# Gate and up products in two passes over x1, and the first normalisation's statistics one slot later: one post-norm layer on one core

## The chip, the cores and the metric

The kernel runs on one core of a Trainium2 chip. TensorE, VectorE (DVE in the rows), ScalarE (ACT), GpSimd (POOL) and SyncE (SP) each work through a queue of their own in order, and meet at semaphores. The metric is the device time of one execution in microseconds. The time before is the median of three runs.

## The reference, cut to what matters

For each of 16 sequences of 256 rows by 256 columns, all in fp32:

```python
qkv = x @ Wqkv + bqkv                      # 16 query heads, 4 key/value heads of 16
prob = softmax(q k^T / 16)
x1 = layernorm(x + (prob v) @ Wout + bout)
gate, up = split(x1 @ ternary(w_gate_up).T)      # 1024 columns each
h = silu(gate) * up
y = rms_norm(h) @ ternary(w_proj).T
out = layernorm(x1 + y)
```

The ternary weights are made in the kernel at its start. Products that need fp32 accuracy are made from two fast ones: an operand is split into a rounded high part and the rest, its low part.

## The kernel before

The work is a pipeline of slots. One sequence takes eight slots of issue, and 172 slots in all are run; sequence b passes through stage `OFFSET` in slot 8b + OFFSET. Slots 0 to 63 and 128 to the end are written out, those between are a hardware loop whose body is 16 slots. A slot is the same list of "if this stage is due" blocks on every engine, so the order of the blocks in an engine's `slot` function is the order of its queue. What is called slot residue r below is the slot whose number is r modulo 8.

Every slot, if its stage is running, does one eighth of the attention of a sequence (two score products for the row maxima, the scores again for the exponential, every second slot the product with v) and one eighth of the feed-forward of an earlier sequence:

- TensorE, `gate_up` (line 507): eight matmuls 128x128 by 128x256 into one PSUM bank `ffn_ps`, gate in one half and up in the other. It waits for `x1T_lo` (the low part of x1 transposed) and for `h_done` of the slot before, since `ffn_ps` is single.
- ScalarE: tanh of the gate half, and behind it in its queue the exponential, then `h_hi` of the slot before.
- DVE: row maximum 0, then `gated` and `h_f` (lines 817 and 824), then row maximum 1.
- GpSimd (line 924 on), first in the slot: `h_lo` and, behind it, the running sum `sq_sum` of the slot before. Then, if due, `LN2_APPLY` (the final output `y_out` of the sequence two before, two instructions), then `RSTD1`, then others.

The first normalisation is made once in eight slots. In residue 3 (offset 27) TensorE makes the output projection; DVE at the end of that slot adds the residual (`r1`, line 890), takes `bn_stats` twice and `bn_aggr` twice; GpSimd, at the end of its slot, makes `rstd1` in two small instructions (lines 944 and 922). In residue 4 (offset 28) DVE, behind row maximum 1, applies it (`LN1_APPLY`, line 881, two instructions that make `x1`). In residue 5 TensorE transposes x1 (line 613; its PSUM bank is the one of that slot's row maximum 0) between the product with v and `down`; ScalarE makes `x1T_hi`. In residue 6 DVE makes `x1T_lo` (line 765) behind `h_f`. In residue 7 the first `gate_up` of the sequence uses both. `LN2_APPLY` has offset 44, so it falls in residue 4 too.

The GpSimd queue around it:

```python
if st := n.once(LN2_APPLY):          # 44
    wait(pool, rstd2_done, st.count(1, 1))
    ...                              # two tensor_scalar of 128x256
if st := n.once(RSTD1):              # 27
    wait(pool, var1_done, st.count(TT, TT))
    pool.tensor_tensor(ve1[:], mv1[:, :, 1], ln_eps[:], ALU.add)
    wait(pool, ve1_done, st.count(1, 1))
    rsqrt(rstd1[:], ve1[:], rstd1_done)
```

Of the kernel before, what the change touches and what calls it, by code (L numbers as in the profile page):

```python
# [24 lines left out]
P = 128  # L25
# [3 lines left out]
F = 4 * D  # L29
TT = S // P  # L30
DT = D // P
# [43 lines left out]
PV_DIVIDE = (22, 24)  # L75
ATT_HIGH = 26
O_ADD = 27
RSTD1 = 27
X1_HIGH = 29
X1_LOW = 30  # L80
GATE0 = 31
# [85 lines left out]
def wait(eng, sem, value):  # L167

    if isinstance(value, int):
        if value > 0:  # L170
            eng.wait_ge(sem, value)
    else:
        eng.wait_ge(sem, value)
# [26 lines left out]
def postln_layer(nc, x, Wqkv, bqkv, Wout, bout, w_gate_up, w_proj, out):  # L200
    ctx = ExitStack()
    with ctx:
        def sb(name, shape, dt=F32):
            return ctx.enter_context(nc.sbuf_tensor(name, shape, dt))
# [4 lines left out]
        def sem(name):  # L209
            return ctx.enter_context(nc.semaphore(name))  # L210
# [14 lines left out]
        wguT = sb("wguT", [P, DT, 2 * F], F32R)  # L225
# [37 lines left out]
        r1 = sb("r1", [P, TT, D])  # L263
        st1 = sb("st1", [P, TT, 6])
        mv1 = sb("mv1", [P, TT, 2])
# [3 lines left out]
        x1T = [sb(f"x1T_{n}", [P, 2, DT, S], F32R) for n in ("hi", "lo")]  # L269
# [23 lines left out]
        def short(n, name):  # L293
# [30 lines left out]
        r1_done, bn1_done, var1_done, ve1_done, rstd1_done, x1_done = (  # L324
            sem("r1_done"), sem("bn1_done"), sem("var1_done"), sem("ve1_done"), sem("rstd1_done"), sem("x1_done"))
        x1_turned, x1T_hi, x1T_lo = sem("x1_turned"), sem("x1T_hi"), sem("x1T_lo")
# [6 lines left out]
        waited, sp_waited, pool_waited = sem("waited"), sem("sp_waited"), sem("pool_waited")  # L333
# [16 lines left out]
        def alternate(n, st):  # L350

            return n.it is None and n.t >= TWO_BANKS and st.s % 2 == 1

        def gate_up_bank(n, st, half):
            return exp_ps[:, half, 0:S] if alternate(n, st) else ffn_ps[:, half, :]
# [86 lines left out]
        def _(pe):  # L442
            def products(dst, lhs, rhs, start=True, stop=True):

                pairs = list(zip(lhs, rhs))
                for i, (a, b) in enumerate(pairs):
                    last = pe.matmul(dst, a, b, start=start and i == 0, stop=stop and i == len(pairs) - 1)  # L447
                return last
# [56 lines left out]
                last.then_inc(exp_scored, 1)  # L505

            def gate_up(n, st):
                wait(pe, x1T_lo, st.count(1, 1))
                if st.it is None and st.b == 0 and st.s == 0:
                    pe.wait_ge(w_ev, len(pieces))  # L510
                if alternate(n, st) and n.t - SLOTS < TWO_BANKS and st.s == 1:
                    wait(pe, exp_done, SLOTS * B)
                wait(pe, h_done, st.count(8, st.s - 1 if n.it is None and n.t > TWO_BANKS else st.s))
                for half in range(2):
                    c = half * F + st.s * P
                    last = products(gate_up_bank(n, st, half),
                                    [wguT[:, k, c:c + P] for k in range(DT) for _ in range(2)],
                                    [x1T[a][:, st.par, k, :] for k in range(DT) for a in range(2)])
                last.then_inc(ffn_made, 1)

            def down(st):
# [48 lines left out]
            def slot(n):  # L570
                if st := n.chunk(FFN0):
                    gate_up(n, st)
# [187 lines left out]
        def _(dve):  # L760
# [3 lines left out]
            def low(dst, src, hi):  # L764
                return dve.tensor_tensor(dst, src, hi.bitcast(F32), ALU.subtract)  # L765

            def both(n, name):
                return short(n, name)[:].rearrange("p (k t) -> p k t", k=2)
# [42 lines left out]
            def slot(n):  # L811
# [7 lines left out]
                if st := n.chunk(H0):  # L819

                    wait(dve, gated_done, st.count(8, st.s + 1))
                    wait(dve, h_lo, st.count(8, st.s - 1))
                    wait(dve, h_squared, st.count(8, st.s - 1))
                    dve.tensor_tensor(h_f[:, st.s % 2, :], gated[:, st.s % 2, :], gate_up_bank(n, st, 0), ALU.mult  # L824
                                      ).then_inc(h_done, 1)
                if st := n.once(X1_LOW):
                    wait(dve, x1T_hi, st.count(1, 1))
                    low(x1T[1][:, st.par], both(n, "x1"), x1T[0][:, st.par]).then_inc(x1T_lo, 1)
# [41 lines left out]
                if st := n.once(V_COPY):  # L870
# [4 lines left out]
                    for t in range(TT):  # L875
                        last = dve.tensor_copy(v_ones[:, st.par, t, :, 0:HD], v[:, t, 1])
# [10 lines left out]
                if st := n.once(O_ADD):  # L887
                    wait(dve, o_made, st.count(1, 1))
                    wait(dve, bout_added, st.count(1, 1))
                    dve.tensor_tensor(r1[:], both(n, "o"), res[:, st.par], ALU.add).then_inc(r1_done, 1)  # L890
                    wait(dve, r1_done, st.count(1, 1))
                    for t in range(TT):
                        dve.bn_stats(st1[:, t, :], r1[:, t, :]).then_inc(bn1_done, 1)  # L893
                    wait(dve, bn1_done, st.count(TT, TT))
                    dve.sem_inc(waited, 1)
                    for t in range(TT):
                        dve.bn_aggr(mv1[:, t, :], st1[:, t, :]).then_inc(var1_done, 1)
                if st := n.once(K_LOW):
                    wait(dve, k_copied, st.count(1, 1))
                    low(k_p[:, 1, :], kv_f[0:KV, :], k_p[:, 0, :]).then_inc(k_lo, 1)  # L900

            run_slots(dve, slot)


        @block.gpsimd
        def _(pool):
# [17 lines left out]
            def slot(n):  # L924
# [10 lines left out]
                if st := n.once(LN2_APPLY):  # L935
# [3 lines left out]
                    for t in range(TT):  # L939
                        pool.tensor_scalar(y_out[:, st.par, t, :], r2[:, t, :], mv2[:, t, 0:1], rstd2[:, t:t + 1],  # L940
                                          ALU.subtract, ALU.mult).then_inc(y_done, 1)
                if st := n.once(RSTD1):
                    wait(pool, var1_done, st.count(TT, TT))
# [53 lines left out]
```

## Time and profile before

| | |
|---|---|
| median of three runs | 621.06 us (619.04 to 621.45) |
| profiled execution | 616.0 us, of it 614.1 us span |
| mean granted TensorE clock | 0.971 |
| TensorE matmul busy | 554.9 us, 90% of the span |
| TensorE weight load busy | 467.1 us, 76% |
| DVE busy | 442.1 us, 72% |
| ScalarE busy | 369.9 us, 60% |
| GpSimd busy | 327.6 us, 53% |

An engine's busy time is a sum over the whole span. Which wait ends last in which slot has to be read from the timeline. Between sequences the steady part repeats every 32.8 us.

### The profile page before, as it was taken

Reading aid. Unit: us, or ns where it says so; the run is one execution under the profiler, and the core shown is the slowest. Engines: PE = TensorE matmul, PEld = TensorE weight load, DVE = VectorE, ACT = ScalarE, POOL = GpSimd, SP = SyncE. Lnnn points to the kernel's source line nnn. Section 1 sums busy time; section 2 is a strip of 40 time slices with the busy share of each in tenths; the row PEclk is TensorE's granted clock in tenths of the full one; section 3 lists DMA queues with packets and bytes.
Section 4 is the critical chain, followed back from the end, with each engine's and each line's share of the span. In section 5 each row is a group of like instructions: output and inputs, shape, how many; then the busy total and the mean of one; then the engine's idle time right before and its main releaser. Section 6 shows DMA issues by size and latency. Waiting matters only on the chain.

```text
span 614.1 us, 14165 instructions
## 1 busy us (share of the span) xinstructions
PE 554.9 (90%) x4368; PEld 467.1 (76%) x4368; DVE 442.1 (72%) x1034; ACT 369.9 (60%) x738; POOL 327.6 (53%) x436
## 2 busy tenths in 40 slices
PE   5768979999999999999999999999999999999782
PEld 5657768778888887878787888788887877777772
DVE  7885875777777777786777777877777787855751
ACT  4453745576666666757566666666666756566441
POOL 5432331243645555555637473646555555566975
PEclk9687999999999999999999999999999999999996
DMA  6963454454352617062534435342617070101001
GB/s 226 159 139 45 84 83 89 79 97 70 77 107 59 124 45 139 4 148 37 136 47 103 78 77 103 78 104 63 119 44 138 23 141 4 36 2 36 18 1 35
DMA packets 53932, 49.08 MB, mean 80 GB/s; under 512 B 6144, under 2 KB 53888, under 8 KB 53888
## 3 DMA queue, kind: packets, MB, share of 16 engines
q1 hardware_dynamic: 51152, 47.60, 37.8%
q10 hardware_dynamic: 2736, 0.92, 0.7%
q8 instruction: 24, 0.39, 0.3%
q14 instruction: 20, 0.16, 0.1%
HBM read 33.29 MB, written 14.68 MB: 78 GB/s over the span
## 4 chain that ended last, share of the span: by engine, by line
PE 68%; DVE 20%; issue 5%; POOL 3%; ACT 1%; DMA 1%; ACTq 0%; POOLq 0%; DVEq 0%; SPq 0%
PE ffn_ps L447 17%; PE short_ps L447 11%; PE pv_ps L544 10%; PE short_ps L494 8%; PE down_ps L529 7%; PE exp_ps L503 7%; PE short_ps L552 5%; DVE w_hat L809 3%; DVE row_max L776 3%; DVE gated L817 2%; DVE st L893 2%; DVE r L890 2%; DVE x1T_lo L765 2%; DVE h_f L824 1%; DVE w_sum L793 1%
## 5 line engine op out<-in xcount | busy, mean ns | idle before, releaser
L776 DVE TENSOR_REDUCE row_max<-short_ps 128x2 f32<-128x512 f32 x256 | 173.7, 682 | 64.5 <-PE short_ps L494 64.4
L928 POOL TENSOR_TENSOR h_lo<-h_f,h_hi 128x256 fp32r<-128x256 f32 x128 | 94.6, 739 | 191.2 <-ACT h_hi L672 180.9
L690 ACT ACTIVATE probs<-exp_ps 128x1024 f32<-128x1024 f32 x128 | 130.9, 1023 | 37.3 <-PE exp_ps L503 34.0
L447 PE MATMUL ffn_ps<-x1T_hi,wguT 128*128 128x256 f32 x480 | 125.0, 293 | 15.9 <-DVE h_f L824 9.0
L494 PE MATMUL short_ps<-k_st,q_st 65*128 65x256 f32 x512 | 116.5, 309 | 13.0 <-DVE row_max L776 12.7
L447 PE MATMUL ffn_ps<-x1T_lo,wguT 128*128 128x256 f32 x480 | 119.3, 282 | 0.0
L681 ACT ACTIVATE tanh<-ffn_ps 128x256 f32<-128x256 f32 x120 | 45.8, 382 | 118.9 <-PE ffn_ps L447 101.9
L447 PEld LDWEIGHTS ffn_ps<-x1T_hi,wguT 128*128 128x128 f32 x480 | 90.8, 189 | 23.0 <-DVE h_f L824 11.1
L494 PEld LDWEIGHTS short_ps<-k_st,q_st 65*128 65x128 f32 x512 | 82.1, 192 | 23.6 <-DVE row_max L776 11.1
L447 PEld LDWEIGHTS ffn_ps<-x1T_lo,wguT 128*128 128x128 f32 x480 | 91.0, 189 | 0.0
L933 POOL TENSOR_TENSOR sq_sum<-sq_sum,h_sq 128x256 f32<-128x256 f32 x112 | 83.2, 743 | 0.0
L529 PE MATMUL down_ps<-wpT,h_hi 128*128 128x256 f32 x256 | 76.2, 320 | 5.9 <-POOL h_lo L928 5.9
L503 PE MATMUL exp_ps<-q_st,k_st 67*128 67x512 f32 x256 | 81.4, 399 | 0.2
L544 PE MATMUL pv_ps<-probs,v_ones 128*32 128x256 f32 x1024 | 68.5, 385 | 0.0
L529 PE MATMUL down_ps<-wpT,h_lo 128*128 128x256 f32 x256 | 66.8, 283 | 0.0
L529 PEld LDWEIGHTS down_ps<-wpT,h_hi 128*128 128x128 f32 x256 | 48.8, 191 | 19.5 <-issue 11.5
L817 DVE SCALAR_TENSOR_TENSOR gated<-tanh,ffn_ps 128x256 f32<-128x256 f32 x120 | 49.3, 410 | 18.9 <-ACT tanh L681 18.9
L824 DVE TENSOR_TENSOR h_f<-gated,ffn_ps 128x256 f32<-128x256 f32 x120 | 50.5, 421 | 5.4 <-DVE gated L817 1.6
L672 ACT ACTIVATE h_hi<-h_f 128x256 fp32r<-128x256 f32 x128 | 52.3, 409 | 1.2 <-DVE h_f L824 1.2
L529 PEld LDWEIGHTS down_ps<-wpT,h_lo 128*128 128x128 f32 x256 | 49.0, 191 | 0.4
L447 PE MATMUL short_ps<-xT,wqkv 128*128 128x256 f32 x192 | 48.2, 388 | 0.0
L722 ACT ACTIVATE h_sq<-h_f 128x256 f32<-128x256 f32 x112 | 45.7, 408 | 0.0
(98 smaller groups left out, 892.7 us busy)
## 6 DMA issues: line engine op xcount, KB each, us to landing
q_st<-q_dram SPq DMA_DIRECT2D x128, 128.0 KB, 4.1
q_dram<-q_p SPq DMA_DIRECT2D x16, 512.0 KB, 3.0
xn<-in_L_attn_x_dram SPq DMA_DIRECT2D x16, 256.0 KB, 4.5
k_st<-k_dram SPq DMA_DIRECT2D x64, 64.0 KB, 2.6
res<-in_L_attn_x_dram SPq DMA_DIRECT2D x16, 256.0 KB, 3.2
out_dram<-y_out SPq DMA_DIRECT2D x16, 256.0 KB, 2.2
wgu_raw<-in_L_ffn_w_gate_up_dram SPq DMA_DIRECT2D x8, 256.0 KB, 6.5
k_dram<-k_p SPq DMA_DIRECT2D x16, 128.0 KB, 3.1
```

What stands on the lines that cost most here:

```text
L447: last = pe.matmul(dst, a, b, start=start and i == 0, stop=stop and i == len(pairs) - 1)
L494: last = pe.matmul(bank[:, t * S:(t + 1) * S], q_st[0:PAD, st.par, head, t * P:(t + 1) * P], k_st[0:PAD, st.par, st.s % 4, :], start=True, ...
L503: last = pe.matmul(exp_ps[:, t, :], k_st[:, st.par, st.s % 4, t * P:(t + 1) * P], q_st[:, st.par, first_head(st.s):first_head(st.s) + 5:4, ...
L529: last = pe.matmul(down_ps[:, t, :], h_p[a][:, st.s % 4, t * P:(t + 1) * P], wpT[:, st.s, :], start=(st.s == 0 and t == 0 and a == 0), sto ...
L544: last = pe.matmul(pv_ps[r:r + 32, s % 4 // 2, :], v_ones[:, st.par, t, s % 4, :], probs[:, s % 4, t, i, :], start=(t == 0), stop=(t == TT ...
L672: return act.activation(dst, src, ACT.Identity)
L690: act.activation(probs[:, st.s % 4], exp_ps[:], ACT.Exp).then_inc(exp_done, 1)
L776: dve.tensor_reduce(row_max[:, st.par, head * TT:(head + 1) * TT], short(n, f"max{i}")[:].rearrange("p (t k) -> p t k", t=TT), AX.X, ALU.m ...
L817: dve.scalar_tensor_tensor(gated[:, st.s % 2, :], tanh[:, st.s % 2, :], 1.0, gate_up_bank(n, st, 1), ALU.add, ALU.mult).then_inc(gated_don ...
L824: dve.tensor_tensor(h_f[:, st.s % 2, :], gated[:, st.s % 2, :], gate_up_bank(n, st, 0), ALU.mult).then_inc(h_done, 1)
L928: pool.tensor_tensor(h_p[1][:, st.s % 4, :], h_f[:, st.s % 2, :], h_p[0][:, st.s % 4, :].bitcast(F32), ALU.subtract).then_inc(h_lo, 1)
L933: pool.tensor_tensor(sq_sum[:, st.par, :], sq_sum[:, st.par, :], h_sq[:, st.s % 2, :], ALU.add).then_inc(h_summed, 1)
```

## The change

Two edits. In `gate_up` the eight matmuls are issued in another order, first the four with the high part of x1 (gate, then up), then the four with the low part, and the wait for the low part moves between them; the first wait is now for the high part. The bank's accumulation is opened once, by the first matmul, except where gate and up lie in two banks. And the statistics of the first normalisation leave the end of slot residue 3 on DVE for residue 4, behind `h_f`; `RSTD1` moves from 27 to 28 on GpSimd, at its old place in the slot's list. `LN1_APPLY` stays at 28.

```diff
+LN1_STATS = 28
-RSTD1 = 27
+RSTD1 = 28
...
             def gate_up(n, st):
-                wait(pe, x1T_lo, st.count(1, 1))
+                wait(pe, x1T_hi, st.count(1, 1))
...
                 wait(pe, h_done, st.count(8, st.s - 1 if n.it is None and n.t > TWO_BANKS else st.s))
-                for half in range(2):
-                    c = half * F + st.s * P
-                    last = products(gate_up_bank(n, st, half),
-                                    [wguT[:, k, c:c + P] for k in range(DT) for _ in range(2)],
-                                    [x1T[a][:, st.par, k, :] for k in range(DT) for a in range(2)])
+                for a in range(2):
+                    if a:
+                        wait(pe, x1T_lo, st.count(1, 1))
+                    for half in range(2):
+                        c = half * F + st.s * P
+                        first = a == 0 and (half == 0 or alternate(n, st))
+                        for k in range(DT):
+                            last = pe.matmul(gate_up_bank(n, st, half), wguT[:, k, c:c + P], x1T[a][:, st.par, k, :],
+                                             start=first and k == 0, stop=a == 1 and k == DT - 1,
+                                             skip_group_check=True)
                 last.then_inc(ffn_made, 1)
...
+                if st := n.once(LN1_STATS):
+                    wait(dve, r1_done, st.count(1, 1))
+                    for t in range(TT):
+                        dve.bn_stats(st1[:, t, :], r1[:, t, :]).then_inc(bn1_done, 1)
+                    wait(dve, bn1_done, st.count(TT, TT))
+                    dve.sem_inc(waited, 1)
+                    for t in range(TT):
+                        dve.bn_aggr(mv1[:, t, :], st1[:, t, :]).then_inc(var1_done, 1)
                 if st := n.once(X1_LOW):
...
                     dve.tensor_tensor(r1[:], both(n, "o"), res[:, st.par], ALU.add).then_inc(r1_done, 1)
-                    wait(dve, r1_done, st.count(1, 1))
-                    for t in range(TT):
-                        dve.bn_stats(st1[:, t, :], r1[:, t, :]).then_inc(bn1_done, 1)
-                    wait(dve, bn1_done, st.count(TT, TT))
-                    dve.sem_inc(waited, 1)
-                    for t in range(TT):
-                        dve.bn_aggr(mv1[:, t, :], st1[:, t, :]).then_inc(var1_done, 1)
```

## Rows read from the trace of the kernel before

**Rows 1.** The page: matmul busy tenths and granted TensorE clock in 40 slices.

```profile
PE   5768979999999999999999999999999999999782
...
PEclk9687999999999999999999999999999999999996
```

**Rows 2.** Chain of waits that ended last, 300 to 370 us: start, length, what.

```profile
327.93 0.77 DVE st L893 x2
...
330.50 1.22 PE ffn_ps L447 x8
...
334.84 0.94 PE ffn_ps L447 x8
```

**Rows 3.** Timeline, slot residues 4 and 5: start us, length us, engine, line [idle before].

```profile
328.84 0.25 DVE L897 BATCH_NORM_AGGREGATE mv<-st 128x2 f32<-128x6 f32 x2 [0.16 <-DVE st L893]
329.01 0.66 DVE L776 TENSOR_REDUCE row_max<-short_ps 128x2 f32<-128x512 f32 x1
...
329.17 0.19 POOL L944 TENSOR_TENSOR ve<-mv,ln_eps 128x2 f32<-128x2 f32 x1 [1.30 <-DVE mv L897]
...
329.44 0.70 POOL L922 TENSOR_TENSOR rstd<-ve,minus_half 128x2 f32<-128x2 f32 x1
...
330.03 0.42 DVE L824 TENSOR_TENSOR h_f<-gated,ffn_ps 128x256 f32<-128x256 f32 x1
...
330.37 0.68 DVE L776 TENSOR_REDUCE row_max<-short_ps 128x2 f32<-128x512 f32 x1
...
330.96 1.41 DVE L881 TENSOR_SCALAR x<-r,mv,rstd 128x256 f32<-128x256 f32 x2
...
331.43 0.79 POOL L933 TENSOR_TENSOR sq_sum<-sq_sum,h_sq 128x256 f32<-128x256 f32 x1
...
332.21 2.47 POOL L940 TENSOR_SCALAR y_out<-r,mv,rstd 128x256 f32<-128x256 f32 x2
...
333.33 0.42 DVE L824 TENSOR_TENSOR h_f<-gated,ffn_ps 128x256 f32<-128x256 f32 x1
...
333.70 0.42 PEld L552 LDWEIGHTS short_ps<-ident,x 128*128 128x128 f32 x4 [0.41 <-issue]
...
334.68 0.28 PE L447 MATMUL ffn_ps<-x1T_hi,wguT 128*128 128x256 f32 x1
```

**Rows 4.** Timeline, residues 6 and 7: the low part of x1 and its first reader.

```profile
337.12 0.42 DVE L824 TENSOR_TENSOR h_f<-gated,ffn_ps 128x256 f32<-128x256 f32 x1
...
337.46 0.68 DVE L765 TENSOR_TENSOR x1T_lo<-short_ps,x1T_hi 128x512 fp32r<-128x512 f32 x1
...
338.27 0.38 PE L447 MATMUL ffn_ps<-x1T_hi,wguT 128*128 128x256 f32 x1 [0.48 <-DVE x1T_lo L765]
```

**Rows 5.** Who waited for the low part of x1, all sequences: us, times.

```profile
  PE ffn_ps L447: 6.9, 15
```

**Rows 6.** GpSimd's final output instructions: ns min/median/max, first and last start.

```profile
L940 POOL TENSOR_SCALAR y_out<-r,mv,rstd x32: 1212/1220/1262, 168.3 to 610.3; 128x256 f32<-128x256 f32 x32
```

**Rows 7.** Timeline: applying the first normalisation for sequences 0, 1 and 15.

```profile
104.72 0.73 DVE L881 TENSOR_SCALAR x<-r,mv,rstd 128x256 f32<-128x256 f32 x2
...
134.38 1.39 DVE L881 TENSOR_SCALAR x<-r,mv,rstd 128x256 f32<-128x256 f32 x2
...
577.08 1.54 DVE L881 TENSOR_SCALAR x<-r,mv,rstd 128x256 f32<-128x256 f32 x2 [0.33 <-POOL rstd L922]
```

**Rows 8.** Timeline near the end: matmuls behind a pause of TensorE.

```profile
595.03 0.38 PE L529 MATMUL down_ps<-wpT,h_hi 128*128 128x256 f32 x1 [2.29 <-POOL h_lo L928]
...
596.42 0.41 PE L447 MATMUL ffn_ps<-x1T_lo,wguT 128*128 128x256 f32 x1
596.63 0.41 PE L447 MATMUL ffn_ps<-x1T_hi,wguT 128*128 128x256 f32 x1
```

**Rows 9.** Half-microsecond stretches: us, PE busy (count), granted clock, DMA share, GB/s.

```profile
595.50:596.00 0.50, 0.50 (x7) 0.91 0.00 0
...
599.00:599.50 0.50, 0.50 (x4) 0.67 0.12 33
```

## The prediction

> **What bounds the kernel now.** I read the page first: TensorE's matmuls fill nine tenths of every slice from the sixth to the thirty-seventh, at the full clock [rows 1]. Next the chain of waits over two sequences of the steady part. It is TensorE nearly throughout, and leaves it for DVE at two places in eight slots: at the end of residue 3 and in 4, where it goes through the statistics, `gated` and `h_f` to the next `gate_up`, and in 6 and 7, where it goes through `x1T_lo` [rows 2, 4]. Those are the two places that the change touches. Last the timeline of residues 4 and 5 on DVE and GpSimd, to see what each queue holds when a statistic arrives a slot later [rows 3]. What counts there is the order: in residue 4 GpSimd makes `sq_sum`, then `y_out`, whose two instructions fill 332.21 to 334.68.
>
> **First edit: the order in gate_up.** Eight matmuls and eight weight loads stay eight; one bank stays one. The wait that is new between the fourth and fifth is satisfied in seven slots of eight. In residue 7 the first matmul starts at 338.27, 0.13 us after `x1T_lo` ends at 338.14; `h_f` had ended at 337.54 [rows 4]. Released by `h_f` alone, `gate_up` is put by the chain 0.05 behind its end (330.45, 330.50) and given 1.22, where it takes 0.94 in the flow [rows 2, 3]; so I let a released matmul start 0.16 behind, between 0.05 and 0.33. The four high-part products then start at 337.70 and are issued by 338.2. The low ones then start when `x1T_lo` is there, 338.27, and end half a `gate_up` earlier: 0.47, and up to 0.1 more since the first matmul behind a wait is longer [0.38 in rows 4]. I take 0.5. DVE has the attention's division before its next row maximum, but TensorE does not wait for it there, the chain stays on TensorE for the two slots after, so the gain is kept. It is waited for in 15 sequences of 16 by name [rows 5], and I count 16: -8.0 us. Bounds: 0.43 a time (6.9 over 16) and 0.6, so -7 to -10.
>
> **Second edit, its gain.** The statistics hold DVE from 327.93 to 329.01 [rows 2, 3]. Without them DVE waits at this place for TensorE's scores, as it does in the slots where it has no such work, so most of the 1.08 us is not won. I give `h_f` and the next `gate_up` 0.13 us, between 0 and 0.3; this is an estimate, and small beside what follows.
>
> **Second edit, its cost.** Now DVE does: `h_f` to 330.32, `bn_stats` from 330.24, `bn_aggr` 0.91 later (327.93 to 328.84) and done by 331.40, row maximum 1 from 331.32 (0.17 behind, as 329.01 behind 328.84) to 332.0. Then `x` needs `rstd1`, and `rstd1` is now made by GpSimd in residue 4. What stands before it in that queue? `h_lo`, `sq_sum`, and `y_out`, which ends at 334.68 [rows 3]. The statistics are there at 331.40 and lie 3.3 us unused. GpSimd then takes 0.27 (`ve1` to `rstd1`) and 0.70, so `rstd1` is done at 335.65, and `x` starts at 335.70 instead of 330.96: 4.74 later, while DVE stands still from 332.0 with row maximum 0, `gated` and `h_f` of residue 5 behind the waiting instruction. `x` takes 1.41; to 337.1. Behind it row maximum 0, 0.68, to 337.7. TensorE's transpose of x1 uses the bank of this row maximum, so it waits for both; 0.13 for the handover gives 337.82, against 333.70 [rows 3]. From there to `gate_up` of residue 6 is TensorE's own work, 0.98 (333.70 to 334.68): 338.80. `h_f` of residue 5, 333.75 before, ends at 338.5 and is not last. So `gate_up` starts 4.1 us later, and the 0.13 is in that number. In residue 6 DVE and ScalarE are again waiting for TensorE, and nothing in the steady part waits for a transfer, so nothing takes the delay back.
>
> How often: `y_out` stands in that slot for the first normalisation of sequences 2 to 15, 14 times; its 32 instructions are all 1.21 to 1.26 long, so the price does not vary [rows 6]. For 2 to 14, 13 x 4.1 = 53.3. For 15, `x` already waits for `rstd1` at 577.08, with GpSimd's queue close behind [rows 7]; the same steps give 3.7. For sequence 1 there is no `y_out`: 2.47 less, 1.7. For sequence 0 GpSimd is empty and only the row maximum and its own 0.97 are passed: 0.7, between 0 and 1.3. Together 59.4.
>
> `x` is taken at 1.41, as long as it is with GpSimd busy beside it; for sequence 0, with GpSimd idle, the two take 0.73 [rows 7]. After the stall GpSimd goes straight on with the next `h_lo`, so I keep 1.41. If it were 0.73 each time the sum would fall by 14 x 0.68 = 9.5, a bound for the low end. The Trainium skill, GPSIMD Engine Reference, section 1 (Specifications), says that GpSimd's memory interfaces are shared with VectorE, which contends with it in some forms; the rows of sequences 0 and 1 agree with it, and by it too 1.41 is the figure here.
>
> **The clock.** TensorE has nothing from about 333.6 to 337.8 in each stall, 4.1 us. The nearest pause in the trace is the 2.29 us before 595.03 [rows 8]. Behind it the granted clock leaves 1.00 within the half-microsecond from 595.5 (mean 0.91, so at 595.9) and is back within that from 599.0 (mean 0.67, so at 599.3): 3.4 us at 0.50, which is 1.2 GHz, with matmuls 0.21 apart where they are 0.12 apart at 2.4 GHz [rows 2, 8, 9]. Steady TensorE work in such a stretch loses half of it, at most 1.7 us. Bounds per stall: 0 and 1.7. The pause here is nearly twice as long as that one, and what follows (transposes, `down`, `gate_up`, scores) is TensorE-bound for 2.1 us at the full clock; a part of the low stretch may lie in the pause itself. I take 1.2: 14 x 1.2 = 16.8.
>
> The Trainium skill, TensorE: Matmul & The Clock Gate, section "HAM oscillation — how this bites in real kernels", tells of a kernel that waited between bursts, fell to the low rate in each wait and paid for it in every burst. By that rule none of the 14 stalls is free, and the sum is mine or up to 7 us more; without it, the sum has no clock term and ends 17 us lower. The pause before 595.03 agrees with the rule.
>
> **The sum.** 59.4 - 8.0 + 16.8 = 68.2. On the profiled execution's own 616.0 us that is 684.2. The median of the runs is 5.1 above that execution (621.06), so I predict 689 us.
>
> **Rivals.**
> 1. The same stall, and the clock stays at 2.4 GHz: 621.1 + 51.4 = 672. For it: in most of the trace, with smaller gaps, the clock holds. Against it: the fall behind 2.29 us. 0.15.
> 2. The stall, but part of it has cover that I do not see, for instance `x` at 0.73 and the low parts of other slots catching up, 1 to 2 us a sequence: 640 to 660. Against it: in residue 6 DVE idles for TensorE already. 0.07.
> 3. The stall and more: the low clock outlasts one stretch, since the slots behind it also have short waits. Another 1 us a stall: 705. 0.06.
> 4. The other side: `rstd1` is ready in time. This happens if GpSimd reaches `RSTD1` before 332.0, when DVE comes to `x`; then only the gains are left, 0.5 + 0.13 a sequence, -10 us: 611. It would need `y_out` to start after `RSTD1`, and the list in the slot says otherwise; `y_out` would have to end 3.7 us earlier than it does. 0.02. A change that does nothing measurable would need gains and stall to cancel, under a fifth of the stall that I find: 0.02.
>
> My forecast (stall with the clock's fall) has 0.68, by itself 679 to 696. The range for all goes down to 662, below rival 1 and `x` at its short length with some clock loss, and up to 703; it leaves out the greater part of rivals 2 and 3 and all of 4. Half a per cent, 3 us, is about what a measurement of this kernel can tell from no change. Slower 0.96, same 0.02, faster 0.02.
>
> **What would show it.** In the profile after: DVE `x` idle before it some 3.6 us with GpSimd's `rstd1` as releaser, about 14 times, 50 us in the list of waits; the transpose of x1 behind it waiting some 4 us; the period 36 to 38 us instead of 32.8; in steady slices TensorE at seven or eight tenths, the clock below 1 in the stretch behind each stall; in residue 7 the high products starting ahead of `x1T_lo`, and the 6.9 us wait for it gone. Wrong if GpSimd's `rstd1` comes before `y_out`; if x1's transpose starts before 335; or if the clock row stays at nines with the period near 36.

## The result, and the profile after

The changed kernel takes 690.11 us (median of 4 runs, 689.74 to 691.44), beside 620.05 us before (4 runs, 618.47 to 621.45): 1.1135 times as long, 95% interval 1.110 to 1.117. It is slower by 70 us; predicted were 689 us.

The page of the changed kernel. These are the matmul tenths, GpSimd's tenths and the granted clock, in slices now 17 us long; they answer to [rows 1].

```profile
span 688.0 us, 14165 instructions
...
PE   6668989999797979799897979797988979797672
...
POOL 5533220445454454626354544546363544455866
PEclk9779999999898999999999999999999999999996
...
PE 53%; POOL 17%; issue 15%; DVE 10%; ACT 3%; DMA 1%; POOLq 1%; ACTq 0%; DVEq 0%
```

The last line above is the chain of waits that ended last. On the page of the kernel before it reads:

```profile
PE 68%; DVE 20%; issue 5%; POOL 3%; ACT 1%; DMA 1%; ACTq 0%; POOLq 0%; DVEq 0%; SPq 0%
```

The solid row of nines is broken by sevens, and GpSimd, which had 3% of the chain before, has 17%. The clock row shows almost nothing: a stretch of a few us at half rate, in a slice of 17, still rounds to 9. Its mean for the whole run says more, 0.931 after 0.971.

The list of waits of the changed kernel (us in total, times, longest) names the place:

```profile
PEld short_ps L559 <- DVE row_max L783: 55.8, 14, 4.5
DVE x L896 <- POOL rstd L930: 52.3, 16, 4.0
...
PE short_ps L559 <- DVE x L896: 9.7, 2, 5.4
```

Sixteen times DVE waits for `rstd1`. Fourteen times TensorE's weight load waits for a row maximum: twelve of these are the stalls of the sequences 2 to 13, 4.5 us each, and two are short, 0.41 and 1.28 us, at the sequences 0 and 1. The stalls of the sequences 14 and 15, where no row maximum stands between, are in the third row. In the list before, TensorE's waits for a row maximum ahead of this transpose are missing; of the other two there is this, 0.6 us in place of 52.3 and 1.7 in place of 9.7:

```profile
PE short_ps L552 <- DVE x L881: 1.7, 1, 1.7
...
DVE x L881 <- POOL rstd L922: 0.6, 2, 0.3
```

The timeline of one such place, slot residues 4 and 5, answers to [rows 3]:

```profile
357.09 0.64 PE L523 MATMUL ffn_ps<-x1T_hi,wguT 128*128 128x256 f32 x4
...
360.77 0.25 DVE L840 BATCH_NORM_AGGREGATE mv<-st 128x2 f32<-128x6 f32 x2 [0.16 <-DVE st L836]
...
361.04 0.74 POOL L941 TENSOR_TENSOR sq_sum<-sq_sum,h_sq 128x256 f32<-128x256 f32 x1
...
361.77 2.44 POOL L948 TENSOR_SCALAR y_out<-r,mv,rstd 128x256 f32<-128x256 f32 x2
...
364.45 0.71 POOL L930 TENSOR_TENSOR rstd<-ve,minus_half 128x2 f32<-128x2 f32 x1
365.12 0.73 POOL L936 TENSOR_TENSOR h_lo<-h_f,h_hi 128x256 fp32r<-128x256 f32 x1
365.19 1.53 DVE L896 TENSOR_SCALAR x<-r,mv,rstd 128x256 f32<-128x256 f32 x2 [3.60 <-POOL rstd L930]
...
366.65 0.68 DVE L783 TENSOR_REDUCE row_max<-short_ps 128x2 f32<-128x512 f32 x1
...
367.38 0.42 PEld L559 LDWEIGHTS short_ps<-ident,x 128*128 128x128 f32 x4 [4.51 <-DVE row_max L783]
...
368.79 1.05 PE L523 MATMUL ffn_ps<-x1T_hi,wguT 128*128 128x256 f32 x4
```

Read it from below. TensorE's transpose of x1 has waited 4.51 us for the row maximum; that stands behind `x`; `x` has waited 3.60 us for `rstd1`; and `rstd1` stands behind `y_out`, though its input was ready at 361.02. In the fourteen sequences 2 to 15 the wait of `x` is 3.58 to 3.60 us thirteen times and 3.95 once (sequence 14), as even as an order of issue makes it. `x` begins at 327.56 and again at 365.19: a period of 37.6 us, where it was 32.8.

The clock in the stretch behind that stall, in half microseconds (us, PE busy, clock, DMA share, GB/s):

```profile
367.00:367.50 0.50, 0.12 (x1) 1.00 0.95 336
367.50:368.00 0.50, 0.50 (x5) 0.81 0.22 72
...
371.00:371.50 0.50, 0.50 (x3) 0.77 0.00 0
```

Here it falls just as TensorE takes up work again and is back 3.4 us later. Read in such steps over the whole run, every one of the 14 stalls has a low stretch in it or behind it, 3.4 us long at twelve and 6.8 at the first two; sequences 0 and 1, which wait 0.54 and 1.17 us, have none.

### The profile page after: what moved, and what is told of

The parts are those of the page before. It is cut to its first block, busy times and chain, and to the rows that moved or that the text cites. A ratio compares the mean times of both kernels' runs of the same rounds, so it can differ in the third digit from the quotient of the medians.

```text
span 688.0 us, 14165 instructions
## 1 busy us (share of the span) xinstructions
PE 577.8 (84%) x4368; PEld 489.8 (71%) x4368; DVE 443.2 (64%) x1034; ACT 370.4 (54%) x738; POOL 326.8 (48%) x436
## 4 chain that ended last, share of the span: by engine, by line
PE 53%; POOL 17%; issue 15%; DVE 10%; ACT 3%; DMA 1%; POOLq 1%; ACTq 0%; DVEq 0%
PE ffn_ps L523 12%; PE down_ps L536 7%; PE short_ps L448 7%; PE short_ps L495 6%; PE exp_ps L504 6%; PE short_ps L559 6%; PE pv_ps L551 5%; POOL y_out L948 5%; POOL h_lo L936 4%; POOL sq_sum L941 3%; DVE row_max L783 3%; DVE w_hat L816 2%; DVE x L896 2%; PE ffn_ps L575 1%; POOL res L960 1%
## 5 line engine op out<-in xcount | busy, mean ns | idle before, releaser
L523 PE MATMUL ffn_ps<-x1T_hi,wguT 128*128 128x256 f32 x480 | 86.6, 306 | 8.2 <-DVE h_f L831 8.2
L536 PE MATMUL down_ps<-wpT,h_hi 128*128 128x256 f32 x256 | 80.8, 335 | 6.0 <-POOL h_lo L936 6.0
L523 PE MATMUL ffn_ps<-x1T_lo,wguT 128*128 128x256 f32 x480 | 82.1, 295 | 1.0 <-DVE x1T_lo L772 1.0
L523 PEld LDWEIGHTS ffn_ps<-x1T_hi,wguT 128*128 128x128 f32 x480 | 70.6, 204 | 12.3 <-issue 7.3
L523 PEld LDWEIGHTS ffn_ps<-x1T_lo,wguT 128*128 128x128 f32 x480 | 70.2, 202 | 1.8 <-DVE x1T_lo L772 1.2
L536 PE MATMUL down_ps<-wpT,h_lo 128*128 128x256 f32 x256 | 71.1, 297 | 0.0
L536 PEld LDWEIGHTS down_ps<-wpT,h_hi 128*128 128x128 f32 x256 | 52.0, 203 | 19.6 <-issue 11.5
L559 PE MATMUL short_ps<-ident,x 128*128 128x128 f32 x64 | 14.2, 360 | 58.8 <-DVE row_max L783 49.1
L896 DVE TENSOR_SCALAR x<-r,mv,rstd 128x256 f32<-128x256 f32 x32 | 22.9, 756 | 52.3 <-POOL rstd L930 52.3
L559 PEld LDWEIGHTS short_ps<-ident,x 128*128 128x128 f32 x64 | 8.9, 176 | 66.1 <-DVE row_max L783 55.8
L679 ACT ACTIVATE h_hi<-h_f 128x256 fp32r<-128x256 f32 x128 | 52.3, 408 | 2.4 <-DVE h_f L831 2.4
```

Of the source, the lines that this page charges most:

```text
L523: last = pe.matmul(gate_up_bank(n, st, half), wguT[:, k, c:c + P], x1T[a][:, st.par, k, :], start=first and k == 0, stop=a == 1 and k == D ...
L536: last = pe.matmul(down_ps[:, t, :], h_p[a][:, st.s % 4, t * P:(t + 1) * P], wpT[:, st.s, :], start=(st.s == 0 and t == 0 and a == 0), sto ...
L559: last = pe.transpose(bank[:, i * P:(i + 1) * P], blk, ident[:])
L679: return act.activation(dst, src, ACT.Identity)
```

## The experiments

Each was run on one chip together with others and with the kernel before; ratios are to those runs.

**The new order of gate_up alone.** The kernel before with the new `gate_up`, nothing else; against the changed kernel it is this, and the statistics back behind `r1`:

```diff
 O_ADD = 27
-LN1_STATS = 28
-RSTD1 = 28
+RSTD1 = 27
```

> The kernel before with the new order of gate_up alone; statistics and rstd1 stay where they were. The theory of the prediction (the split lets four products of residue 7 run ahead of x1T_lo): 16 x 0.5 us less, 612 us beside 620, ratio 0.987, and the wait for x1T_lo (6.9 us, 15 times) gone. Rival (the order itself costs TensorE something, a part of the loss of the whole change lies here): 620 us or more.

Measured: 611.73 us (6 runs), ratio 0.9847, interval 0.981 to 0.988. The end of residue 6 in this kernel, beside [rows 4]:

```profile
337.64 0.68 DVE L771 TENSOR_TENSOR x1T_lo<-short_ps,x1T_hi 128x512 fp32r<-128x512 f32 x1
...
337.81 0.71 PE L522 MATMUL ffn_ps<-x1T_hi,wguT 128*128 128x256 f32 x4
...
338.37 0.75 PE L522 MATMUL ffn_ps<-x1T_lo,wguT 128*128 128x256 f32 x4
...
338.96 0.40 PE L494 MATMUL short_ps<-k_st,q_st 65*128 65x256 f32 x2
```

Four high products run while DVE still makes the low part (ready at 338.32); the scores behind `gate_up` start 0.64 us after it is ready. Before, eight products stood between and the distance was 1.17 (338.14 to 339.31). That is 0.53 us a sequence. Over ten sequences of the steady part `x` comes every 32.27 us, where it came every 32.77: 0.50 us a sequence, 8.0 in 16. This is the fastest kernel of the study.

**The move of the statistics alone.** The changed kernel with the old `gate_up`.

```diff
-                wait(pe, x1T_hi, st.count(1, 1))
+                wait(pe, x1T_lo, st.count(1, 1))
...
+                    last = products(gate_up_bank(n, st, half),
...
```

> The move of the statistics and of rstd1 alone, with gate_up as before. The theory of the prediction: all of the loss and the 8 us that the split gives back, 620 + 59.4 + 16.8 = 696 to 698 us. Rival (a part of the loss comes from the new order of gate_up): below 688 us.

Measured: 698.85 us, ratio 1.124 (1.120 to 1.128), 8.7 us above the whole change, 6.6 by the difference of the ratios. All of the loss, and more, is in this part. The distance is not the split's gain alone: in this kernel's trace the low stretch lasts 6.8 us at seven of the 14 stalls, where it does so at two in the changed kernel.

**The order without the earlier start.** High before low, but the wait for the low part ahead of all eight.

```diff
+                wait(pe, x1T_lo, st.count(1, 1))
                 wait(pe, h_done, ...)
                 for a in range(2):
-                    if a:
-                        wait(pe, x1T_lo, st.count(1, 1))
                     for half in range(2):
```

> The kernel before with the four high products ahead of the four low ones, but with the wait for the low part still ahead of all eight. If the gain of the split is the wait's place alone: no change, 619 to 621 us. If the order has a gain or cost of its own (weights, accumulation group): 3 us or more to either side.

Measured: 620.4 us (12 runs), ratio 1.000 (0.997 to 1.003). The order costs and gives nothing that can be measured; the place of the wait is the gain.

**rstd1 ahead of y_out.** The changed kernel with two blocks of GpSimd's queue exchanged.

```diff
+                if st := n.once(RSTD1):
+                    ...
                 if st := n.once(LN2_APPLY):
                     ...
-                if st := n.once(RSTD1):
-                    ...
```

> The changed kernel with the block of rstd1 ahead of the block of y_out in GpSimd's queue, behind sq_sum; all else equal. The theory (y_out in front of rstd1 is 2.44 us of the stall): 14 x 2.44 = 34 us back, 656 us, and if TensorE's pause, then 1.7 us, leaves the clock alone, another 17: 639 us. Rival (rstd1 was late for another reason, such as the statistics themselves): 685 us or more.

Measured: 630.19 us, ratio 1.017 (1.010 to 1.024): 60 us back, where 34 to 51 were expected. Its timeline, and below it the durations of `x` in the sequences 2 to 15 (min/median/max ns):

```profile
341.16 0.70 POOL L930 TENSOR_TENSOR rstd<-ve,minus_half 128x2 f32<-128x2 f32 x1
341.85 1.27 POOL L953 TENSOR_SCALAR y_out<-r,mv,rstd 128x256 f32<-128x256 f32 x1
341.89 0.65 DVE L896 TENSOR_SCALAR x<-r,mv,rstd 128x256 f32<-128x256 f32 x1 [1.13 <-POOL rstd L930]
...
343.52 0.42 PEld L559 LDWEIGHTS short_ps<-ident,x 128*128 128x128 f32 x4 [1.49 <-DVE row_max L783]
```

```profile
L896 DVE TENSOR_SCALAR x<-r,mv,rstd x28: 399/526/652, 174.8 to 592.5; 128x256 f32<-128x256 f32 x28
```

`x` waits 1.13 us in place of 3.60 and TensorE 1.49 in place of 4.5, and the clock stays at 1.00 behind 13 of the 14 stalls. What the expectation left out is the length of `x`. Its two instructions take 0.65 and 0.41 us here, 0.97 together, where they took 1.53; beside them GpSimd now runs `y_out` and not `h_lo`. 14 x 2.44 for the queue, 14 x 0.56 for `x` and 16 for the clock (13 stalls, at the price that the fill below gives) are 58 us, and 60 were measured. What is left is the cost of the moved statistics themselves: TensorE's 1.49 us stand where 0.41 stood before.

**rstd1 first of all.** The same block at the head of GpSimd's slot, ahead of `h_lo`.

```diff
+                if st := n.once(RSTD1):
+                    ...
                 if st := n.chunk(H_LOW0):
```

> The changed kernel with the block of rstd1 first in GpSimd's slot, ahead of h_lo too. rstd1 is then done 1.0 us behind the statistics and DVE waits about 0.5 us. TensorE's transpose still comes some 0.9 us later than before the change, since the statistics stand on DVE ahead of x: 620 + 16 x 0.9 - 8 = 626 us. If h_lo, now held back until the statistics are there, holds down and with it TensorE: 10 us more. Rival (with rstd1 first the move of the statistics pays, 0.13 us a sequence beside the split's gain): 611 us.

Measured: 631.83 us, ratio 1.020 (1.014 to 1.026).

```profile
341.64 0.70 POOL L930 TENSOR_TENSOR rstd<-ve,minus_half 128x2 f32<-128x2 f32 x1
342.31 0.73 POOL L941 TENSOR_TENSOR h_lo<-h_f,h_hi 128x256 fp32r<-128x256 f32 x1
342.38 1.55 DVE L896 TENSOR_SCALAR x<-r,mv,rstd 128x256 f32<-128x256 f32 x2 [0.51 <-POOL rstd L930]
...
344.59 0.42 PEld L559 LDWEIGHTS short_ps<-ident,x 128*128 128x128 f32 x4 [1.45 <-DVE row_max L783]
```

DVE waits only 0.51 us, as expected, but `x` is long again with `h_lo` beside it, and TensorE waits 1.45 us. That is 1.04 more than the 0.41 before the change, where 0.9 more was expected. Even with nothing of GpSimd's ahead of `rstd1` the moved statistics cost: this kernel has the split's gain in it and is 20 us above the kernel that has the split alone. The rival in which the move pays with `rstd1` first is out.

**Filling the stall, too much.** The changed kernel with matmuls of the identity, that nothing reads, ahead of the transpose of x1.

```diff
+                if n.once(X1_T) and (st := n.chunk(EXP0)):
+                    wait(pe, exp_done, st.count(8, st.s + 1))
+                    for _ in range(FILL):            # 32
+                        pe.matmul(exp_ps[:, 0, 0:P], ident[:], ident[:], start=True, stop=True)
                 if st := n.once(X1_T):
```

> The changed kernel with 32 small matmuls of the identity, whose result nobody reads, in TensorE's queue ahead of the transpose of x1, in 13 of the 14 stalls; they wait for the exponential of that slot and take about 3.5 of the 4.1 us that TensorE has nothing. The stall by GpSimd's queue is untouched. The theory with the clock term: the granted clock stays at 1.00 behind these stalls and 13 x 1.2 us come back, 674 us. Rival (the low clock costs nothing that slack does not cover): 690 us with the clock at 1.00. Rival (the fill itself delays the transpose): more than 690.

Measured: 725.83 us, ratio 1.167. The third case of the expectation: I had priced a filling matmul at 0.11 us, and it takes twice that; each is recorded as two. The fill also ran for the sequences 0 and 1, which have no such stall to hide it in, so it came 15 times and not the 13 of the expectation.

```profile
386.16 7.41 PE L623 MATMUL exp_ps<-ident 128*128 128x128 f32 x64
```

The fill ends at 393.4, 3.2 us after the row maximum that the transpose needs. As a test of what the clock costs it failed, since it replaced the stall with a longer one.

**Filling it with half.** FILL is 16, and only for the sequences 2 to 14.

```diff
-                if n.once(X1_T) and (st := n.chunk(EXP0)):
+                if n.once(X1_T) and (st := n.chunk(EXP0)) and (n.it is not None or n.t >= LN2_APPLY):
```

> As the kernel that filled the stall with 32 matmuls, but with 16, and only for the sequences 2 to 14 that have the stall. In that run one filling matmul took 0.226 us (7.24 us for 32), so that the fill outlasted the stall by 3.2 us; 16 take 3.6 us of the 4.1. The theory with the clock term: clock at 1.00 behind these 13 stalls, 13 x 1.2 us back, 674 us. Rival (the low clock costs nothing on the path): 690 us with the clock at 1.00.

Measured: 674.03 us, ratio 1.086 (1.079 to 1.093): 16.1 us under the changed kernel (17 by the difference of the ratios). `x` waits for `rstd1` exactly as long as there (52.3 us in 16 times), and the clock over a whole period is full:

```profile
360.00:372.00 12.00, 11.76 (x98) 1.00 0.64 119
372.00:384.00 12.00, 12.00 (x96) 1.00 0.04 10
384.00:396.00 12.00, 11.62 (x98) 1.00 0.48 98
```

So the stall was there and its clock loss was not: the clock is 16.1 / 13 = 1.24 us a stall. The rival of a free fall of the clock is out.

The price can also be read stall by stall, as the distance from one `x` to the next. First the changed kernel, then this one, sequences 2 and 3:

```profile
175.92 1.53 DVE L896 TENSOR_SCALAR x<-r,mv,rstd 128x256 f32<-128x256 f32 x2 [3.60 <-POOL rstd L930]
...
214.34 1.53 DVE L896 TENSOR_SCALAR x<-r,mv,rstd 128x256 f32<-128x256 f32 x2 [3.60 <-POOL rstd L930]
```

```profile
177.48 1.54 DVE L901 TENSOR_SCALAR x<-r,mv,rstd 128x256 f32<-128x256 f32 x2 [3.60 <-POOL rstd L935]
...
213.80 1.54 DVE L901 TENSOR_SCALAR x<-r,mv,rstd 128x256 f32<-128x256 f32 x2 [3.59 <-POOL rstd L935]
```

That is 38.42 less 36.32, 2.1 us. The next stall gives 1.8. These are the two whose low stretch is 6.8 us long. The other eleven, with 3.4, give 1.0 to 1.5 us each, and all 13 together 17.9. The medians give less in part because the stall of sequence 15, which is not filled, has a low stretch of 6.8 us in this kernel's trace and of 3.4 in the changed kernel's.

**h_lo waits for x.** The changed kernel with GpSimd held in the slot behind until `x` is made.

```diff
+                if st := n.once(LN1_APPLY + 1):
+                    wait(pool, x1_done, st.count(TT, TT))
                 if st := n.chunk(H_LOW0):
```

> The changed kernel with one wait more: in the slot behind, GpSimd begins h_lo only when DVE has finished x. In the changed kernel x takes 1.53 us beside h_lo and sq_sum, and 0.74 us in the two sequences where GpSimd is idle. If GpSimd's two-input products beside it are what makes x long: x takes 0.75 in all sequences and 14 x 0.8 = 11 us come back, 679 us. Rival (x is long for another reason, or the later h_lo holds down): 690 us or more.

Measured: 684.06 us (674.24 to 688.89, 4 runs). `x` is short in all sequences, but the time scatters by 15 us where the changed kernel scatters by 2, and with it the mean granted clock, from 0.935 in the shortest run to 0.903 in the longest. So this experiment alone decides nothing.

```profile
L896 DVE TENSOR_SCALAR x<-r,mv,rstd x32: 406/411/416, 104.9 to 642.6; 128x256 f32<-128x256 f32 x32
```

The clock of a stretch behind one stall shows why:

```profile
359.00:360.00 1.00, 0.00 (x0) 0.99 0.00 0
360.00:361.00 1.00, 0.00 (x0) 0.50 0.56 197
...
366.00:367.00 1.00, 1.00 (x7) 0.60 0.00 0
```

Here the clock falls inside the pause, and stays low for 6.8 us, where 3.4 was the rule before. In the profiled run that holds at 11 stalls of 14, and its low stretches add up to 118 us, against 95 in the changed kernel. The steady part repeats every 37.5 us (`x` at 360.20 and 397.70), as good as unchanged from the 37.6 of the changed kernel, although TensorE's stall is 0.8 us shorter.

**Both: h_lo waits for x, and a fill of 13.**

```diff
+FILL = 13
...
+                if st := n.once(LN1_APPLY + 1):
+                    wait(pool, x1_done, st.count(TT, TT))
```

> The last two edits together: h_lo waits for x, and TensorE fills the stall, with 13 matmuls (2.9 us) since the stall is then 0.8 us shorter. With h_lo waiting alone x was short (0.41 us each) but the low clock lasted 6.8 us behind most stalls in place of 3.4, which ate the gain in most runs. Theory (the short x is worth 0.8 us a stall once the clock is held): 674 - 11 = 663 us, with little scatter. Rival (x is not on the path): 674 us.

Measured: 662.18 us (659.63 to 664.13), ratio 1.064 (1.058 to 1.070). 11.9 us under the fill alone (13.8 by the difference of the ratios), 0.85 a stall, and the scatter is down to 4.5 us. The steady part repeats every 35.5 us, so the 6.8 us stretches cost the kernel before this one 2.0 us a stall. `x` beside `h_lo` and `sq_sum`, instructions of GpSimd with two tensor inputs, was on the path, and the clock had hidden its price in the experiment before.

## Why the prediction was right, point by point

**The place.** As predicted, `rstd1` stands behind `y_out` in GpSimd's queue, DVE stands at `x` with the next row maximum, `gated` and `h_f` behind it, and TensorE cannot transpose x1. Exchanging two blocks of one queue took back 60 of 70 us, so this is shown.

**The stall.** Measured from the first `gate_up` product of residue 4, the transpose came at 6.2 us before (about 327.48 to 333.70) and at 10.29 after (357.09 to 367.38): 4.1 us later, as predicted. Over the run it can be summed sequence by sequence from two traces in which the clock is at 1.00 there, the kernel with half the fill and the one with the split alone, by how much more the transposes of x1 fall behind in each: 1.4 us for sequence 1, 54.4 for 2 to 14 and 3.7 for 15, in all 59.5, where 1.7, 53.3 and 3.7, in all 58.7, were predicted. Ahead of the first transpose the traces of these kernels differ by several us among themselves (it begins between 106.8 and 114.2), so the 0.7 us of sequence 0 is not tested. One term was too small: I took `x` at 1.41 us, and it is 1.53 beside `h_lo` and `sq_sum`. It does not show in the typical stall, since `rstd1` was done 8.07 us behind that first product, where I had 8.17. That `x` is long because of what GpSimd does beside it, and that this is worth 0.85 us a stall, the last experiment shows.

**The split.** Predicted -8.0 us; -9.5 by the kernel that has it alone (interval 7 to 12), -8.0 by the distance between sequences in its trace, and -6.6 to -8.7 by the kernel that lacks it, where the clock differs too. All but the lowest of these lie within the predicted 7 to 10.

**The clock.** Predicted 1.2 us a stall and 16.8 in all; measured 1.24 by the medians, 17.4 for 14, and by the distances 17.9 for 13. It was taken from one pause of the trace before, behind which the low stretch lasted 3.4 us. The rule of the Trainium skill that stood beside it (TensorE: Matmul & The Clock Gate, "HAM oscillation — how this bites in real kernels") held too: none of the 14 stalls was free. Where filling matmuls held the clock, the loss was gone. That the low stretch would be 3.4 us at most stalls was luck. At the first two it was 6.8, and they cost 2.1 and 1.8 us, above the prediction's upper bound of 1.7 a stall. That is what its third rival described, at two stalls of 14. With the stall 0.8 us shorter it was 6.8 at most of them, 2.0 us each.

**The sum.** 68.2 predicted, 70.1 between the medians. On the profiled executions it is 74 (616.0 and 689.7), since the one of before was among its fastest runs. The traces show where: the first `x` begins at 104.72 before and at 108.62 after, and in the changed kernel's trace the clock is low for 3.4 us from about 81 and again from about 91, where it is at 1.00 in the one before. From the first `x` to the end it is 509.4 and 579.4 us, 70.0 more. So the sum was 2 us short, and that 689 meets the median within 1 us is in part chance: the four runs of the kernel before span 3 us.

**The signs.** Most of what I named is in the trace as I named it: a wait of `x` of 3.6 us, 52.3 us in all for 50; a period of 37.6 us in 36 to 38; TensorE's slices at seven to nine tenths in turn, where I had seven or eight; TensorE's wait for `x1T_lo` down from 6.9 us to 1.0. One sign was named badly: I wrote that the clock's row of the page would have to leave its nines. It hardly does. The half-microsecond stretches show what slices of 17 us do not.

**The statistics' own gain.** The 0.13 us a sequence was put down as small and could not be told from nothing; with the stall mostly removed the move still costs.

## What to carry to other kernels

A step that moves one slot later on one engine is queued anew on every engine that serves it: write down what stands ahead of it there, since an engine at 53% busy can hold a 1 us result for 3 us. A stall of TensorE costs its own length plus the clock behind it, here 4.1 us and between 1.0 and 2.1; look for that in stretches as short as the stall. And where two edits come together, time each alone: here a gain of 9 us was hidden under a loss of 79.

## What the runs showed of the hardware that was not expected

- What GpSimd runs beside a DVE `tensor_scalar` from memory to memory (128x256, fp32) sets its time. With GpSimd idle it took 0.41 us. Beside GpSimd's `tensor_tensor`, which has two tensor inputs, it took 0.80 (`h_lo`, then `sq_sum`). Beside GpSimd's `tensor_scalar`, which has one (`y_out`), the first of two took 0.65 and the second 0.41, both while the same GpSimd instruction ran.
- A shorter stall can cost more clock: with pauses of 3.7 us in place of 4.5 the low stretches were mostly 6.8 us and not 3.4, and single runs of that kernel lay between 674 and 689 us. It goes with where the clock falls. In the two traces the stretch was 6.8 us long at the 13 stalls where the clock fell 1.4 to 2.3 us ahead of their end, and 3.4 at the 15 where it fell less than 0.8 ahead of the end or behind it. What sets the moment of the fall is not shown.
- A 128x128 fp32 matmul of the identity takes 0.226 us at the full clock (386.16 to 393.41, 7.25 us for 32), nearly twice the 0.12 of a 128x256 product of the rounded fp32 type.
